# Value products of a head group: four places between score units, or one run behind the fifth unit

## The chip, the cores and the metric

The kernel runs on one NeuronCore of a Trainium2 chip. The metric is the device time of one execution in microseconds (us). The engines are called PE (TensorE, matmuls), PEld (its weight loads), DVE (VectorE), ACT (ScalarE), POOL (GpSimd) and SP (which here only issues DMAs).

## The reference

The input is 16 sequences of 512 rows of 256 floats. What is computed, cut to what matters for the change:

```
xn = layernorm(x)                                   # 16 x 512 x 256
q, k = low-rank projections of xn, 16 heads of 16   # each through rank 64
v = xn @ v_w.T + v_b
att = softmax(where(causal, q @ k.T / 4, min))      # per head, 512 x 512
y = (att @ v) @ o_w.T + o_b
x + y + ffn(xn)    # ffn: 8 experts, each picks its 128 best rows per sequence, silu MLP 256-512-256
```

## The kernel before

The program has two parts. The first does layernorm, attention and the ranking of rows for the experts (up to about 850 us of the span), the second the experts. The change is in the first part.

**Groups and slots.** The 16 sequences (b) have 4 head groups each (g), of 4 heads: 64 groups, G = 4b + g. The work is written out by hand as *slots*, one for each group; `slot_steps` (L56) lists the steps of a slot. All engines run through the same list of steps in the same order, and each does its own part of a step, held by semaphores. Two sequences (eight slots) are the body of a hardware loop (`program`, L338). In what follows "first" to "fourth slot" are g = 0 to 3 of one sequence, and four slots together are a *batch*.

**Units.** A slot has 10 units (u0 to u9). In each unit come, in this order: `scoret` of group G+1 (L877: transposed scores of 512 columns into one of two PSUM banks, which ACT turns into probabilities, L565, and of which POOL clears the diagonal blocks, L469), `score` of group G+3 (L858: scores of 512 columns into one of three PSUM banks, of which DVE takes row maxima, L719), then the steps that two hand-written tables give for that unit. `SUMS` (L49) has the steps of the softmax and the value products, `PROJECTIONS` (L39) the projections of this and later sequences. Those of `SUMS` come first in a unit.

**Waits of PE.** `score` of a unit waits until DVE has reduced the unit three before (L862, three banks). `scoret` waits until ACT has done the unit two before (L881). A shared pair of banks serves all other steps in turn (L797, `await_units` L780).

**Value products.** `pv` k (L892) multiplies the four heads' probabilities of key block k (128 keys, 512 - 128k query columns, fp32) by their values with a column of ones, each head on its own 32 columns of the PE array, and adds up in one PSUM bank over k = 0 to 3. Step 0 waits for POOL (L897) and for the copy of the group before (L903). Step 3 signals `pv_ready` (L913); ACT then copies the bank to `yraw` (L567 to L569), at the place of step 3 in its own list.

**Other steps in `SUMS`.** `maxt` (L870) transposes the negated row maxima of group G+2 on PE, also into 32 columns of the array, and ACT copies them. `maxd` (L553) is ACT's DMA of that copy. `ytr` (L914) transposes `yraw`; DVE normalises (L743, L749).

**Steps of `PROJECTIONS`.** `xt`, `qk_first`, `qk` (both L776), `v`, `yt`, `o` use PE, then ACT (upper half) and DVE (lower half, L588; for `o` the sum with the residual, L756). `mid` turns q and k into bf16 parts on ACT (L541) and POOL (L460), and SP stacks them by 6 DMAs for each of q and k (L400). Behind them SP loads x of a later sequence (`xload`, L382), for which DVE waits in `lnstat` (L655), the last step of the first slot. The first `score` of the second slot is the first that needs the new stack (L864).

Per unit, the steps with PE work besides the scores, `pv`, `maxt` and `ytr`: first slot u0 v, u1 yt, u6 yt, u8 v, u9 v; second u0 v, u2 o, u5 o, u6 o, u8 o; third u0 xt, u1 xt, u6 qk_first, u8 qk, u9 qk_first; fourth u0 qk, u4 qk_first, u6 qk, u8 qk_first, u9 qk.

The order inside one unit is this loop:

```
    for t in range(UN):
        out += [("scoret", G + 1, t)] * (G + 1 < NG) + [("score", G + 3, t)] * (G + 3 < NG) + put[t]
```

Of the kernel before, what the change touches and what calls it, by code (L numbers as in the profile page):

```python
# [25 lines left out]
def unit_parts(t, transposed):  # L26
# [20 lines left out]
     (8, "qk_first", 2, 3), (9, "qk", 2, 3)])  # L47

SUMS = (  # L49
# [4 lines left out]


def slot_steps(b, g):  # L56
# [1125 lines left out]
```

## Time and profile before

| | |
|---|---|
| median of 3 runs | 1301.3 us (1298.12 to 1302.88) |
| the profiled execution, its own time | 1300.67 us |
| its span, first to last instruction | 1298.8 us |
| mean granted TensorE clock | 0.972 of full speed |
| PE busy | 1196.6 us (92%) |
| DVE busy | 965.2 us (74%) |
| ACT busy | 669.8 us (52%) |
| POOL busy | 691.7 us (53%) |

The profile has a page of totals, and a trace that can be asked for stretches. A timeline row has the start in us from the beginning of the span, the duration in us, the engine, the source line, the operation, the tiles it writes and reads, shapes and number of instructions; in brackets the idle time of the engine before it and what ended it. PE's matmuls are pipelined: each row's duration includes the way through the array, so the time that an instruction costs PE is read from one start to the next, not from durations.

### The profile page before, as it was taken

The numbers are of one execution on the slowest core, as the hardware profiler recorded it, in microseconds if no ns is written. First come the engines' busy times: TensorE is split into PE (matmuls) and PEld (weight loads), VectorE is DVE, ScalarE is ACT, GpSimd is POOL, SyncE is SP. The second block draws the span as 40 slices with busy tenths as digits, with TensorE's granted clock in tenths as the row PEclk, the third lists the DMA queues.
The fourth block names the chain that finished last, engine by engine and source line by source line (L and its number), as shares of the span: only waits on it lengthen the run. The fifth ranks groups of instructions, "written<-read, shape, count | busy, mean of one in ns | idle before, by whom it ended". The sixth has DMA issues, their size and how long they took to land. (4 is left out here: it accounts for less than half of the span.)

```text
span 1298.8 us, 29459 instructions
## 1 busy us (share of the span) xinstructions
PE 1196.6 (92%) x8502; PEld 799.1 (62%) x8502; DVE 965.2 (74%) x3293; ACT 669.8 (52%) x1312; POOL 691.7 (53%) x1021
## 2 busy tenths in 40 slices
PE   6799999999999999999999998769999999999995
PEld 5544545555545555555555543348988888888885
DVE  3588878878878878878878879935766656666662
ACT  2357667667667667667667665522332323233220
POOL 1235354355354355345345343344888888888885
PEclk9779999999999999999999999969999999999998
DMA  5443443443443443443443442132555555555454
GB/s 140 114 115 83 116 115 100 116 115 98 114 115 98 114 115 98 114 115 98 114 115 98 114 98 67 34 109 42 108 101 93 117 88 107 93 101 109 85 78 53
DMA packets 106287, 130.31 MB, mean 100 GB/s; under 512 B 21580, under 2 KB 75476, under 8 KB 106196
## 3 DMA queue, kind: packets, MB, share of 16 engines
q1 hardware_dynamic: 76356, 94.46, 27.9%
q0 software_dynamic: 24576, 33.57, 15.7%
q10 hardware_dynamic: 5264, 1.32, 0.5%
q8 instruction: 27, 0.44, 0.1%
q14 instruction: 64, 0.52, 0.1%
HBM read 44.84 MB, written 33.55 MB: 60 GB/s over the span
## 5 line engine op out<-in xcount | busy, mean ns | idle before, releaser
L719 DVE CUSTOM_DVE_ANT_0 junk<-bank,rowmask 128x256 bf16<-128x256 f32 (+3 forms) x1024 | 454.3, 485 | 67.8 <-PE bank L866 42.2
L565 ACT ACTIVATE probs<-bank 128x512 f32<-128x512 f32 x640 | 376.6, 598 | 176.8 <-PE bank L887 175.5
L469 POOL TENSOR_SCALAR_AFFINE_SELECT probs<-probs 128x256 f32<-128x256 f32 (+1 forms) x640 | 223.6, 362 | 315.2 <-ACT probs L565 313.4
L866 PE MATMUL bank<-kstk,qstk 96*128 96x256 bf16 (+3 forms) x1024 | 250.3, 306 | 27.4 <-DMA kstk<-qk_part 13.4
L887 PE MATMUL bank<-qstk,kstk 98*128 98x256 bf16 (+3 forms) x1024 | 252.0, 308 | 3.4 <-ACT probs L565 2.4
L1049 POOL DMA_INDIRECT out_rows<-mixed,rows x128 | 208.5, 1629 | 58.2 <-issue 38.4
L908 PE MATMUL bank<-probs,vaug 128*32 128x512 f32 (+3 forms) x2048 | 193.8, 450 | 6.0 <-POOL probs L469 6.0
L1078 ACT ACTIVATE hid<-bank 128x512 f32<-128x512 f32 x128 | 76.5, 598 | 228.7 <-PE bank L1141 172.4
L887 PEld LDWEIGHTS bank<-qstk,kstk 98*128 98x128 bf16 x1024 | 76.6, 98 | 161.3 <-ACT probs L565 98.5
L1157 PE MATMUL bank<-w_hi,hid_hi 128*128 128x256 f32 x512 | 147.2, 288 | 0.0
L1157 PE MATMUL bank<-w_hi,hid_lo 128*128 128x256 f32 x512 | 144.9, 283 | 0.0
L1157 PE MATMUL bank<-w_lo,hid_hi 128*128 128x256 f32 x512 | 144.8, 283 | 0.0
L866 PEld LDWEIGHTS bank<-kstk,qstk 96*128 96x128 bf16 x1024 | 89.8, 99 | 65.6 <-DVE rowmax L719 26.2
L1109 DVE TENSOR_SCALAR mixed<-bank,gate_sel 128x256 f32<-128x256 f32 x128 | 56.1, 480 | 93.1 <-PE bank L1157 85.4
L460 POOL TENSOR_TENSOR qk_part<-rest,qk_part 128x512 bf16<-128x512 f32 x64 | 74.5, 1164 | 58.1 <-ACT qk_part L541 55.2
L1157 PEld LDWEIGHTS bank<-w_lo,hid_hi 128*128 128x128 f32 x512 | 98.2, 192 | 0.0
L1157 PEld LDWEIGHTS bank<-w_hi,hid_hi 128*128 128x128 f32 x512 | 98.1, 192 | 0.0
L1157 PEld LDWEIGHTS bank<-w_hi,hid_lo 128*128 128x128 f32 x512 | 98.1, 192 | 0.0
L1098 DVE CAST hid_hi<-hid 128x512 fp32r<-128x512 f32 x128 | 55.4, 433 | 49.7 <-ACT hid L1078 31.7
L1100 DVE TENSOR_TENSOR hid_lo<-hid,hid_hi 128x512 fp32r<-128x512 f32 x128 | 89.0, 695 | 4.4
L719 DVE DVE_READ_ACCUMULATOR2_ANT rowmax<- 128x1 f32 x1024 | 85.0, 83 | 0.0
L1141 PE MATMUL bank<-pt_hi,w_hi 128*128 128x512 f32 x256 | 81.0, 398 | 3.9 <-DVE pt_lo L1094 3.9
(131 smaller groups left out, 2060.5 us busy)
## 6 DMA issues: line engine op xcount, KB each, us to landing
qstk<-qk_part SPq DMA_DIRECT2D x96, 256.0 KB, 4.7
kstk<-qk_part SPq DMA_DIRECT2D x96, 256.0 KB, 4.7
xln<-in_L_attn_hidden_states SPq DMA_DIRECT2D x16, 512.0 KB, 6.1
xn_rows<-xn SPq DMA_DIRECT2D x16, 512.0 KB, 3.0
xres<-in_L_attn_hidden_states SPq DMA_DIRECT2D x16, 512.0 KB, 3.6
out_rows<-xres SPq DMA_DIRECT2D x16, 512.0 KB, 2.9
qstk<-in_L_ffn_w SPq DMA_DIRECT2D x8, 512.0 KB
kstk<-in_L_ffn_w SPq DMA_DIRECT2D x8, 512.0 KB
```

Of the source, the lines that this page charges most:

```text
L460: nc.gpsimd.tensor_tensor(qk_part[2][:, k, :], rest[k % 2][:], qk_part[1][:, k, :], ALU.subtract).then_inc(lo_done, 1)
L469: nc.gpsimd.affine_select(out=block, in_=block, compare_op=ALU.is_ge, fill=0.0, base=0, pattern=[[0, len(cols)], [1, P]], channel_multipli ...
L565: nc.scalar.activation(probs[n % 2][:, 512 * k:512 * k + 512], SCORET[k % 2][:], ACT.Exp, scale=SCALE).then_inc(exp_done, 1)
L719: last = nc.vector.tensor_tensor_reduce(out=junk[k % 2][:, col:col + width], in0=SCORE[score_bank(UN * n + k)][:, col:col + width], in1=ro ...
L866: last = nc.tensor.matmul(SCORE[score_bank(UN * n + k)][:, col:col + width], qstk[b % 2][0:KS, GH * g + h, P * i:P * i + P], kstk[b % 2][0 ...
L887: last = nc.tensor.matmul(SCORET[k % 2][:, col:col + width], kstk[b % 2][0:KS + SHIFT, GH * g + h, P * j:P * j + P], qstk[b % 2][0:KS + SH ...
L908: last = nc.tensor.matmul(Y[2 * HD * h:2 * HD * h + 2 * HD, P * k:T], vaug[b % 2][:, k, GH * g + h, :], probs[n % 2][:, col:col + width], ...
L1049: nc.gpsimd.indirect_dma_start(out=out_rows, out_offset=bass.IndirectOffsetOnAxis(ap=moe.rows[:, GB4 * grp + j, e:e + 1], axis=0), in_=mix ...
L1078: nc.scalar.activation(hid[k % 2][:], UP[k][:], ACT.Silu).then_inc(silu_done, 1)
L1100: nc.vector.tensor_tensor(hid_lo[n % 2][:, k, :], hid[k % 2][:], hid_hi[n % 2][:, k, :], ALU.subtract).then_inc(hid_done, 1)
L1141: last = nc.tensor.matmul(UP[k][:], a[:, dt, f], b[:, dt, :], start=m == 0 and dt == 0, stop=m == 2 and dt == DT - 1)
L1157: last = nc.tensor.matmul(DOWN[k][:, D * t:D * t + D], a, b, start=m == 0, stop=m == len(todo_mm) - 1)
```

## The change

Each of the four rows of `SUMS` belongs to one slot of a batch. The entry (unit, kind, groups ahead, k) says where a step stands. The change moves `pv` 0, 1 and 3; `pv` 2, `maxt`, `maxd` and `ytr` keep their units.

```
 SUMS = (
-    [(2, "pv", 0, 0), (3, "maxt", 2, 0), (3, "pv", 0, 1), (4, "maxd", 2, 0), (4, "pv", 0, 2), (5, "pv", 0, 3), (7, "ytr", 0, 0)],
-    [(2, "pv", 0, 0), (3, "maxt", 2, 0), (3, "pv", 0, 1), (4, "maxd", 2, 0), (4, "pv", 0, 2), (6, "pv", 0, 3), (7, "ytr", 0, 0)],
-    [(2, "pv", 0, 0), (3, "maxt", 2, 0), (3, "pv", 0, 1), (4, "maxd", 2, 0), (4, "pv", 0, 2), (5, "pv", 0, 3), (7, "ytr", 0, 0)],
-    [(2, "pv", 0, 0), (3, "maxt", 2, 0), (3, "pv", 0, 1), (4, "maxd", 2, 0), (4, "pv", 0, 2), (5, "pv", 0, 3), (7, "ytr", 0, 0)])
+    [(3, "maxt", 2, 0), (4, "pv", 0, 0), (4, "pv", 0, 1), (4, "maxd", 2, 0), (4, "pv", 0, 2), (4, "pv", 0, 3), (7, "ytr", 0, 0)],
+    (the same row three more times)
```

`maxd` has no PE part, so on PE the sixteen products of a group stand in one run behind the fifth score unit (u4). In the fourth slot `qk_first` of u4 follows the run. All waits stay as written.

## Rows read from the trace of the kernel before

**Rows 1.** The page: busy time, share of the span, instructions
```profile
PE 1196.6 (92%) x8502; PEld 799.1 (62%) x8502; DVE 965.2 (74%) x3293; ACT 669.8 (52%) x1312; POOL 691.7 (53%) x1021
```

**Rows 2.** Busy time by stretch: PE, PEld, DVE, ACT, POOL, granted clock, DMA
```profile
400.00:500.00 100.00, 97.24 (x759) 53.25 (x756) 85.04 (x351) 68.81 (x140) 43.99 (x95) 1.00 0.43 111
```

**Rows 3.** Who waited for whom, 100 to 740 us: total us, times, longest
```profile
PE bank L866 <- DMA kstk<-qk_part: 11.0, 10, 1.6
PE bank L866 <- DVE rowmax L719: 5.2, 6, 1.1
```

**Rows 4.** Timeline of PE, third slot of a batch, u2 to u6
```profile
445.43 0.38 PE L866 MATMUL bank<-kstk,qstk 96*128 96x256 bf16 x2
445.74 1.07 PE L908 MATMUL bank<-probs,vaug 128*32 128x512 f32 x8
446.74 0.39 PE L887 MATMUL bank<-qstk,kstk 98*128 98x512 bf16 x1
446.96 0.38 PE L866 MATMUL bank<-kstk,qstk 96*128 96x512 bf16 x1
447.28 0.23 PE L874 MATMUL bank<-ident_bf,negmax 128*32 128x128 bf16 x1
447.29 0.86 PE L908 MATMUL bank<-probs,vaug 128*32 128x384 f32 x8
448.08 0.39 PE L887 MATMUL bank<-qstk,kstk 98*128 98x384 bf16 x2
...
449.74 0.43 PE L908 MATMUL bank<-probs,vaug 128*32 128x128 f32 x8
450.09 0.39 PE L887 MATMUL bank<-qstk,kstk 98*128 98x384 bf16 x2
```

**Rows 5.** Timeline of DVE, third slot: end of u0, end of u1, u2, u5
```profile
446.36 0.08 DVE L719 DVE_READ_ACCUMULATOR2_ANT rowmax<- 128x1 f32 x1
...
447.65 0.08 DVE L719 DVE_READ_ACCUMULATOR2_ANT rowmax<- 128x1 f32 x1
...
448.25 0.41 DVE L719 CUSTOM_DVE_ANT_0 junk<-bank,rowmask 128x256 bf16<-128x256 f32 x1
...
450.23 0.68 DVE L719 CUSTOM_DVE_ANT_0 junk<-bank,rowmask 128x512 bf16<-128x512 f32 x1
```

**Rows 6.** Timeline of PE and DVE, fourth slot, u2 to u6
```profile
407.93 0.38 PE L866 MATMUL bank<-kstk,qstk 96*128 96x256 bf16 x2
...
408.64 0.08 DVE L719 DVE_READ_ACCUMULATOR2_ANT rowmax<- 128x1 f32 x1
...
409.93 0.08 DVE L719 DVE_READ_ACCUMULATOR2_ANT rowmax<- 128x1 f32 x1
...
411.13 0.64 PE L908 MATMUL bank<-probs,vaug 128*32 128x256 f32 x8
...
411.70 0.50 PE L776 MATMUL bank<-xt_hi,wqk_hi 128*128 128x512 f32 x1
...
412.51 0.39 PE L887 MATMUL bank<-qstk,kstk 98*128 98x512 bf16 x1
...
413.33 0.69 DVE L719 CUSTOM_DVE_ANT_0 junk<-bank,rowmask 128x512 bf16<-128x512 f32 x1 [1.14 <-PE bank L866]
413.40 0.39 PE L887 MATMUL bank<-qstk,kstk 98*128 98x384 bf16 x2
```

**Rows 7.** Timeline, boundary from first to second slot: PE, then DVE
```profile
431.66 0.39 PE L866 MATMUL bank<-kstk,qstk 96*128 96x512 bf16 x1 [1.26 <-DMA kstk<-qk_part]
...
432.71 0.75 DVE L657 BATCH_NORM_STATS2 stats<-xln 128x6 f32<-128x256 f32 x2 [1.81 <-DMA xln<-in_L_attn_hidden_states]
```

**Rows 8.** Timeline, first slot at a turn of the loop: DVE u0, PE u3, DVE u5
```profile
471.15 0.69 DVE L719 CUSTOM_DVE_ANT_0 junk<-bank,rowmask 128x512 bf16<-128x512 f32 x1 [2.76 <-issue]
...
471.90 0.39 PE L866 MATMUL bank<-kstk,qstk 96*128 96x512 bf16 x1 [1.05 <-DVE rowmax L719]
...
475.04 0.69 DVE L719 CUSTOM_DVE_ANT_0 junk<-bank,rowmask 128x512 bf16<-128x512 f32 x1
```

3 rows, old and new, of the table SUMS are left out of this document.

## The prediction

> **What bounds the kernel now.** I began with the page. PE is busy 92% of the span, DVE 74% [rows 1]. That is an average over two parts, so I asked for stretches. Within the attention part PE is busy 97 of 100 us and DVE 85, at full granted clock [rows 2]. The experts' part isn't touched, and I leave it at what it takes.
>
> Next I read who waited for whom. Between 100 and 740 us PE waits 5.2 us for DVE's row maxima and 11.0 us for the stack DMA (ten waits, of at most 1.6 us) [rows 3]. So PE sets the pace almost everywhere, and once per batch a transfer does. But DVE has only 15% to spare and feeds back on PE through three score banks. The question is whether PE still finds a free bank when the order changes, and that has to be read from timelines.
>
> I followed one batch: third slot [rows 4, 5], fourth slot [rows 6], the boundary between first and second [rows 7], and a first slot at a turn of the loop [rows 8]. The reader should see there how late DVE runs: the u3 score starts at 446.96, and the reduction of u0, whose bank it takes, ended only at 446.44 [rows 4, 5].
>
> **What the change removes on PE.** Starts are compared. A block of products costs 1.00, 0.79 and 0.35 us for 512, 384 and 128 columns [rows 4], 0.57 for 256 [rows 6]. The last two differ by 128 columns and 0.22, so streaming is close to 1.7 ns a column, 0.85, 0.64, 0.43 and 0.21 us, together 2.13; about 0.15 us remains at the end of each block. At the beginning, the score before a block costs 0.31 [rows 4], where a bf16 unit of 512 columns costs 0.22 (446.74 to 446.96) [rows 4]: 0.09 more. Where `qk_first` follows a block of 256 columns, it starts 0.57 after it, and the next scoret comes 0.81 later [rows 6]: 1.38 less 0.43 of streaming leaves 0.95 for exit and `qk_first` together.
>
> PE enters and leaves the narrow shape (32 columns a head) four times per slot now. `maxt` shares one of these stretches: it starts 0.01 before pv 1 [rows 4]. Afterwards `maxt` stands alone (0.09 + 0.05 of streaming + 0.15 = 0.29) and the run is one stretch (0.09 + 2.13 + 0.15, and I add 0.03 for three inner boundaries = 2.40). Old: 4 x 0.24 + 2.13 + 0.01 = 3.10. New: 2.69. **PE has 0.4 us per slot less to do.** The trace has no boundary between two blocks of products. Its cost lies between 0.01 (maxt to pv 1, same shape) and 0.15 (the full exit). I take 0.01, as the nearest row is one within the narrow shape, and keep 0.15 for the range.
>
> The Trainium skill, TensorEngine Tiling (Array Packing), section Tiling Modes, says that a change of tiling mode drains TensorE. By that rule alone the change only gains; the 0.09 and 0.15 above agree with it. It is the first rival's mechanism below.
>
> **What else moves.** No DMA moves, and SP and POOL keep their lists. The select that pv 0 waited for has two more units of time. On ACT the `yraw` copy now stands right after the exponential of u4 (behind `maxd`, which stays ahead of it) and waits for the run's end, with the exponential of u5 behind it. That costs nothing: scoret of u5 comes after the run anyway, and the first waiter is scoret of u7, over 1.2 us after the run; an ACT operation takes 0.51 on average (669.8 / 1312) [rows 1]. If u6 had no projection as cover, it could cost some 0.2 a slot.
>
> **What the change adds: PE meets the banks early, then starves DVE.** Third slot, both engines taken to start as before (in the second slot DVE is behind from its wait for x [rows 7], works without a break, and `o` and `ytr` wait for it, so PE can't gain there).
> - Scoret of u3 starts at 445.43 + 0.22 = 445.65, its score could start at 445.87, but needs u0's reduction, 446.44 [rows 5] plus 0.06 (the release seen in [rows 8], 471.84 to 471.90) = 446.50. **Stall 0.6.**
> - The score ends at 446.72, maxt alone 447.01, scoret of u4 447.24. The score of u4 needs u1's reduction, 447.73 + 0.06 = 447.79 [rows 5]. **Stall 0.55.** It ends at 448.01.
> - The run ends at 450.41, and u5 at 450.86. Before, u6 started at 450.09 [rows 4]. **PE is 0.77 late.**
> - DVE needs 1.98 us for u2 to u4 (448.25 to 450.23) [rows 5], is done at 450.23 and gets u5 at about 451.2, so it idles 1 us where it had none. From u5 on PE works through without a stall, as before, so all that follows is 0.7 to 0.8 late.
>
> Fourth slot, everything 0.77 later:
> - scoret of u3 at 407.93 + 0.22 + 0.77 = 408.92, the score wanted at 409.15, allowed at 408.72 + 0.77 + 0.06 = 409.55 [rows 6] (stall 0.4); maxt ends 410.06; the score of u4 wanted at 410.29, allowed at 410.01 + 0.83 = 410.84 (stall 0.55), done 411.06.
> - The run without its exit takes 2.25, exit and `qk_first` 0.95, u5 0.45: u6 starts at 414.7 instead of 413.40 [rows 6]. That is 1.3 late in all. PE is seldom as exactly placed as in a sum of starts, and only a reading that errs towards a stall is hidden in it, so **I take 1.2 per batch.** DVE's idle time before u5 grows from 1.14 [rows 6] to over 2.
>
> First and second slot. The split of the last `qk` of the fourth slot is what `mid`, the stack DMAs and the load of x follow from. It is 1.2 late, so the stack and x arrive 1.2 late [rows 7]. PE and DVE waited 1.26 and 1.81 there, which covers what the run does within the first slot (PE gains 0.4 and waits it again). So the batch grows by 1.2, not by more. In the second slot DVE is behind from its wait for x, and the run costs it nothing. At a turn of the loop DVE starts 2.76 late and PE waits 1.05 [rows 8]: there u5's score comes at 471.90 + 0.22 + 0.29 + 0.45 + 2.40 + 0.23 = 475.5, and DVE starts it at 476.1 instead of 475.04, so 1.0 late. The wait for x covers some of it: 1.81 in [rows 7], but less here, where DVE starts late; I take 0.65 and leave 0.35.
>
> **Sum.** 14 sequences with the whole structure (b = 0 to 13; the last two have no `qk` left) x 1.2 = 16.8; 6 turns of the loop x 0.35 = 2.1; the last two sequences about 1 (DVE has rank steps between u3, u4 and u5, which fill most of the gap). Together **+20 us**. The profiled execution took 1300.67 us and the median is 1301.3, 0.6 above, so the forecast for the median is **1321 us** (+1.5%).
>
> **Rivals.**
> 1. *Faster: PE keeps what the fewer exits give.* Decides if DVE's reductions of u0 and u1 end before PE wants their banks, or if DVE catches up. Per batch, the last three slots gain 0.4 each, the first nothing for its DMA: 14 x 1.2 = 17 less, 1284 us. For it: PE is busy 97%, DVE 85% [rows 2]. Against it: DVE's times in [rows 5, 6] leave PE 0.5 us of room at u3, and the change takes away pv 0 ahead of it, 1.1 us with its entry. Chance 0.10.
> 2. *No change.* The stalls are there, but DVE's lateness is caught up in gaps of the fourth and first slot (1.26 at the DMA alone [rows 7]), if the stack isn't as late as the split. Then stalls and gain cancel: 1301 us. Against it: between u5 of the fourth slot and the stack everything hangs on PE's own order. Chance 0.13.
> 3. *Slower still: inner boundaries cost 0.15 each.* The run takes 2.82 instead of 2.40, in third and fourth slot (0.84 a batch, 12 us) and, 0.2 each, at the loop's turns (1 us): 1334 us. For it: weights of the next block's four heads can't be seen loading ahead in the trace. Against it: [rows 4], maxt to pv 1. Chance 0.15.
>
> The forecast has 0.62. Half a per cent, 6.5 us, is about what a measurement of this kernel can tell. Slower by more than that: forecast and rival 3, 0.77, and a small part of rival 2, so 0.78. Within it: 0.12. Faster: rival 1, 0.10. The forecast's own range, with 0.15 to 0.2 us of reading error in each stall, is 1311 to 1330. The range goes to 1303 below, into rival 2, and to 1336 above, over rival 3. Rival 1 and half of rival 2 stay out.
>
> **What the new profile would show.** PE: in the third slot the u3 and u4 scores each with an idle time before them that ends by DVE, about 0.5 us; the total "PE waits for DVE row maxima" up from 5 us to some 25 to 30 (13 batches x 2.1). The run's four blocks 2.4 us from first start to next scoret; 2.8 means rival 3. DVE: idle 1 us before u5 in the third slot and 2 in the fourth. The wait for the stack DMA no shorter than now. A batch 1.2 us longer than now. The forecast is wrong if the stalls at u3 and u4 are missing, or if they are there and the next batch's stack still lands at the old pace. The experts' part should not change.

## The result and the profile after

| | before | after |
|---|---|---|
| median | 1301.4 us (4 runs) | 1344.99 us (1342.63 to 1347.15, 4 runs) |
| ratio | | 1.034, 95% interval 1.0315 to 1.0364 |
| span of the profiled execution | 1298.8 us | 1345.2 us |
| mean granted clock | 0.972 | 0.958 |
| us lost to a clock under full, from the first `ytr` to the last | 6.8 | 25.6 |

The change costs 44 us, where 20 were forecast: the sign was right, the size less than half. (The last row sums one less the granted clock over the time. From the first to the last `ytr` is nearly all of the attention part.)

The page after. The second line is the granted clock in tenths, in 40 slices; it answers to [rows 1] with its busy times.

```profile
PE 1193.4 (89%) x8502; PEld 833.3 (62%) x8502; DVE 962.8 (72%) x3293; ACT 660.8 (49%) x1312; POOL 691.6 (51%) x1021
...
PEclk9779999999999989999999998877999999999998
```

PE does the same instructions in 3 us less busy time, in a span 46 us longer. The stretch that answers to [rows 2]:

```profile
400.00:500.00 100.00, 91.09 (x695) 52.74 (x694) 76.59 (x317) 61.64 (x128) 42.06 (x90) 0.95 0.41 103
```

PE fell from 97 to 91 us of 100, DVE from 85 to 77, and the clock is no longer full. What PE waited for between 100 and 740 us (answers to [rows 3]):

```profile
PE bank L887 <- ACT probs L565: 20.6, 34, 0.8
PE bank L866 <- DVE rowmax L719: 17.9, 21, 2.3
PE bank L866 <- DMA kstk<-qk_part: 8.8, 7, 1.8
```

The waits for DVE came, 18 us for 5, though fewer than the 25 to 30 that the prediction looked for. The largest wait is one that [rows 3] hasn't: `scoret` waits 20.6 us for ACT's exponentials (2.4 us in the whole kernel before).

The third slot, PE (answers to [rows 4]), from scoret of u3 to scoret of u5, and then DVE at u5 (answers to [rows 5]):

```profile
412.48 0.39 PE L887 MATMUL bank<-qstk,kstk 98*128 98x512 bf16 x1
413.32 0.39 PE L866 MATMUL bank<-kstk,qstk 96*128 96x512 bf16 x1 [0.45 <-DVE rowmax L719]
414.00 0.22 PE L874 MATMUL bank<-ident_bf,negmax 128*32 128x128 bf16 x1 [0.28 <-DVE xt_lo L588]
414.16 0.39 PE L887 MATMUL bank<-qstk,kstk 98*128 98x384 bf16 x2
414.61 0.39 PE L866 MATMUL bank<-kstk,qstk 96*128 96x384 bf16 x2
414.93 2.36 PE L908 MATMUL bank<-probs,vaug 128*32 128x512 f32 x32
417.23 0.39 PE L887 MATMUL bank<-qstk,kstk 98*128 98x512 bf16 x1
```
```profile
418.05 0.69 DVE L719 CUSTOM_DVE_ANT_0 junk<-bank,rowmask 128x512 bf16<-128x512 f32 x1 [0.91 <-PE bank L866]
```

The score of u3 could have started 0.22 after its scoret, at 412.70, and started at 413.32: 0.6 late, as forecast. The idle time in brackets is shorter than the delay, since the matmul before is still shown running for a part of it. The run takes 2.30 us to the next scoret, DVE idles 0.91 before u5 (1 forecast). This slot went as worked out.

The fourth slot (answers to [rows 6]), PE from the u2 score to the u5 scoret:

```profile
423.91 0.38 PE L866 MATMUL bank<-kstk,qstk 96*128 96x256 bf16 x2
425.09 0.39 PE L887 MATMUL bank<-qstk,kstk 98*128 98x512 bf16 x1 [0.80 <-ACT probs L565]
425.32 0.38 PE L866 MATMUL bank<-kstk,qstk 96*128 96x512 bf16 x1
425.63 0.23 PE L874 MATMUL bank<-ident_bf,negmax 128*32 128x128 bf16 x1
426.36 0.39 PE L887 MATMUL bank<-qstk,kstk 98*128 98x384 bf16 x2 [0.50 <-ACT probs L565]
426.59 0.43 PE L866 MATMUL bank<-kstk,qstk 96*128 96x384 bf16 x2
426.94 3.95 PE L908 MATMUL bank<-probs,vaug 128*32 128x512 f32 x32
430.83 0.50 PE L776 MATMUL bank<-xt_hi,wqk_hi 128*128 128x512 f32 x1
```

Two things differ from the forecast. The scoret of u3 was due at 424.13 (0.22 after the score before it) and comes 0.96 later, that of u4 was due at 425.79 (0.16 after `maxt`, as in the third slot) and comes 0.57 later, both held by ACT. And the run takes 3.89 us to the next row, not the 2.3 that it takes in the third slot and in ten of the fourteen fourth slots. ACT in that time:

```profile
423.43 0.60 ACT L537 ACTIVATE qk_part<-bank 128x512 bf16<-128x512 f32 x1 [0.31 <-PE bank L776]
423.93 0.62 ACT L541 ACTIVATE qk_part<-rest 128x512 bf16<-128x512 f32 x1
424.45 0.59 ACT L565 ACTIVATE probs<-bank 128x512 f32<-128x512 f32 x1
425.19 0.63 ACT L541 ACTIVATE qk_part<-rest 128x512 bf16<-128x512 f32 x1 [0.15 <-DVE rest L588]
425.73 1.07 ACT L565 ACTIVATE probs<-bank 128x512 f32<-128x512 f32 x2
```

The exponential of u1 (424.45), whose bank scoret of u3 needs, stands behind the split of the projection and the copy of `mid`; that of u2 (425.73) behind a second copy. In the kernel before, ACT's order was the same and PE didn't wait, because pv 0 stood ahead of the scoret of u3 and gave ACT the time. There (fourth slot of [rows 6]) the exponential of u1 ends at 409.06, and that scoret follows at 409.24 without idle time:

```profile
408.47 0.59 ACT L565 ACTIVATE probs<-bank 128x512 f32<-128x512 f32 x1
409.24 0.39 PE L887 MATMUL bank<-qstk,kstk 98*128 98x512 bf16 x1
```

The granted clock around that run, by stretches of 1 us (after the length: PE, PEld, DVE, ACT, POOL, clock, DMA):

```profile
424.00:425.00 1.00, 0.29 (x3) 0.01 (x1) 1.00 (x3) 1.00 (x3) 0.37 (x1) 1.00 0.00 0
425.00:426.00 1.00, 0.77 (x3) 0.27 (x3) 1.00 (x6) 0.85 (x3) 1.00 (x2) 1.00 0.00 0
426.00:427.00 1.00, 0.64 (x8) 0.32 (x12) 1.00 (x5) 1.00 (x4) 1.00 (x2) 0.90 0.00 0
427.00:428.00 1.00, 1.00 (x9) 0.34 (x12) 0.91 (x6) 0.41 (x1) 1.00 (x4) 0.50 0.00 0
428.00:429.00 1.00, 1.00 (x12) 0.20 (x4) 0.01 (x2) 0.00 (x0) 0.25 (x1) 0.50 0.30 68
429.00:430.00 1.00, 1.00 (x12) 0.26 (x8) 0.00 (x0) 0.00 (x0) 0.00 (x0) 0.50 0.98 297
```

PE idles 1.3 of 3 us in these waits, and then the clock is at its lower level, 0.50 (1.2 GHz), through most of the run, the densest work there is. It doesn't happen each time: PE idles 1.2 to 1.3 us in the 4 us before the run in all fourth slots of the first fourteen sequences, and 4 of these 14 runs met the low clock. So did one run in a first slot and five of the seven last ones. Why just these isn't known.

DVE meanwhile has no score for 4.45 us, and the waits at the boundary between first and second slot (answers to [rows 7]) are only 0.15 us shorter than they were:

```profile
432.46 0.69 DVE L719 CUSTOM_DVE_ANT_0 junk<-bank,rowmask 128x512 bf16<-128x512 f32 x1 [4.45 <-PE bank L866]
...
451.36 0.75 DVE L657 BATCH_NORM_STATS2 stats<-xln 128x6 f32<-128x256 f32 x2 [1.66 <-DMA xln<-in_L_attn_hidden_states]
```
```profile
450.30 0.39 PE L866 MATMUL bank<-kstk,qstk 96*128 96x512 bf16 x1 [1.11 <-DMA kstk<-qk_part]
```

**Pace.** From the timelines I took when PE starts `ytr` in each of the 64 slots, and the steps between these starts. Typical values of slots without a clock drop, us (the last two lines are experiments that come below):

```
                                 4th>1st  1st>2nd  2nd>3rd  3rd>4th   batch
before          loop not turning   11.64    14.47    10.56    11.76   48.4
                loop turning       12.8     13.4     10.51    11.74   48.5
after           loop not turning   11.73    14.25    11.33    12.78   50.1
                loop turning       13.36    13.04    11.26    12.78   50.4
run behind u2   loop not turning   11.57    14.86    10.42    11.24   48.1
mid at u3       loop not turning   11.73    14.28    11.33    12.10   49.4
```

A batch is 1.7 us longer at full clock, 2.0 at a turn of the loop, 7 x 1.66 + 7 x 1.99 = 25.6 us. With the clock drops, the first fourteen sequences are 37.6 us longer (716.0 for 678.4, first `ytr` to the first of the fifteenth), the last two 9.1 (89.4 for 80.2). The low clock lost (in the sense of the table's last row) 11.9 us in the first of these stretches, where it lost nothing before, and 13.7 in the second, for 6.8 before. So in the first stretch 12.0 us are left beyond the 25.6, and the clock has 11.9 for them. One of these drops, at 143.5 us, isn't at a run; it comes within 1 us of a wait of 1.78 us for the stack DMA.

### The profile page after: what moved, and what is told of

Same layout as the page of the kernel before. It is cut to its first block and busy times, and to the rows that moved or that the text cites. A ratio compares the mean times of both kernels' runs of the same rounds, so it can differ in the third digit from the quotient of the medians.

```text
span 1345.2 us, 29459 instructions
## 1 busy us (share of the span) xinstructions
PE 1193.4 (89%) x8502; PEld 833.3 (62%) x8502; DVE 962.8 (72%) x3293; ACT 660.8 (49%) x1312; POOL 691.6 (51%) x1021
## 5 line engine op out<-in xcount | busy, mean ns | idle before, releaser
L565 ACT ACTIVATE probs<-bank 128x512 f32<-128x512 f32 x640 | 367.5, 599 | 80.1 <-PE bank L887 79.0
L908 PE MATMUL bank<-probs,vaug 128*32 128x512 f32 (+3 forms) x2048 | 168.5, 474 | 4.9 <-POOL probs L469 4.9
L887 PEld LDWEIGHTS bank<-qstk,kstk 98*128 98x128 bf16 x1024 | 79.8, 99 | 111.7 <-ACT probs L565 54.7
L908 PEld LDWEIGHTS bank<-probs,vaug 128*32 128x32 f32 x2048 | 63.9, 117 | 106.4 <-issue 90.4
L569 ACT ACTIVATE yraw<-bank 128x512 f32<-128x512 f32 x64 | 38.3, 598 | 151.2 <-PE bank L908 151.2
```

The source lines that it names most:

```text
L565: nc.scalar.activation(probs[n % 2][:, 512 * k:512 * k + 512], SCORET[k % 2][:], ACT.Exp, scale=SCALE).then_inc(exp_done, 1)
L887: last = nc.tensor.matmul(SCORET[k % 2][:, col:col + width], kstk[b % 2][0:KS + SHIFT, GH * g + h, P * j:P * j + P], qstk[b % 2][0:KS + SH ...
L908: last = nc.tensor.matmul(Y[2 * HD * h:2 * HD * h + 2 * HD, P * k:T], vaug[b % 2][:, k, GH * g + h, :], probs[n % 2][:, col:col + width], ...
```

## Experiments

Theory A, after this reading: PE meets u3 and u4 too early, waits there for DVE and (fourth slot) ACT, and this idle time lets the clock fall in runs behind it. The rival theories (B to E) stand in the expectations. Medians below are to be held against 1345.0 us for the changed kernel. Fillers are extra matmuls that PE runs in its waits: their result is overwritten, and all outputs are still computed.

**One slot's row taken back.** The edits put the old row of `SUMS` back at its place:

```
e1_fourth_back:     rows new, new, new, old
e2_third_back:      rows new, new, old, new
e3_first_two_back:  rows old, old, new, new
```

> Only the fourth slot gets its old row back; the other three keep the run behind u4. Theory A (two causes: PE stalls on DVE and ACT around u3 and u4, and in the fourth slot the clock falls to half during the run, since PE stood idle just before it): in the changed kernel's trace the step from the third to the fourth slot's ytr is 1.0 us longer than before, and in four of fourteen batches 2.6 us. Taking that back gives 14 x 1.0 + 4 x 1.6 = 20 us and some of the clock losses at the end, about 1320 to 1325 us. Theory B (the run as such is dearer than four blocks, in every slot alike): a quarter of 44 us, about 1334 us. Theory C (my prediction's reading, stalls of the third and fourth slot only at full clock, 1.3 against 0.8): about 1337 us.

Measured: 1327.2 us, ratio 1.0206 (1.0183 to 1.0229): 18 us back by one slot of four. Theory B, equal shares (1334 us), is out, and so is theory C, the prediction's own reading (1337 us).

> Only the third slot gets its old row back. Theory A: the step from second to third slot's ytr is 0.7 us longer in the changed kernel, 14 x 0.7 = 10 us, so about 1333 to 1336 us, with the clock drops of the fourth slot still there. Theory B: 1334 us as well, so this run alone does not part A from B; with the run before it does. Theory C: 14 x 0.8 = 11 us, 1334 us.

Measured: 1341.6 us, 1.0313 (1.0293 to 1.0332), a miss for all: 3 us back, not 10. The step from second to third slot is 10.5 again. But the clock now fell in seven fourth slots of the first fourteen sequences (3rd>4th at 14.4 to 14.6 instead of 12.8) and in two first slots. In these sequences it lost 18.8 us, for 11.9 in the changed kernel. What the third slot gave, 14 x 0.75 = 10.5 us, went to the clock for the most part. So the effects of single slots don't add up.

> First and second slot get their old rows back, third and fourth keep the run. Theory A: DVE's and PE's waits for the stack DMA and for x cover these two slots except where the loop turns (0.55 us longer, 6 times, and one clock drop of two windows there), so 3 to 7 us less: 1338 to 1342 us. Theory B: half of 44 us less, about 1323 us.

Measured: 1342.8 us, 1.0312 (1.0295 to 1.033). Theory B (1323 us) is out, and theory A's range is missed by 0.8 us. The first two slots are covered: at full clock a batch takes 50.2 us, for 50.1 and 50.4 in the changed kernel. The clock fell in six fourth slots here.

**Fillers: is it the clock?** The numbers of fillers per place are given in the expectations; `filler` looks them up.

```
+  if filler(kind, n, k):
+      pe.wait_ge(yraw_done, at(n - 3, 8))          # n - 1 ahead of scoret
+  for _ in range(filler(kind, n, k)):
+      nc.tensor.matmul(Y[:], wqk_hi[:, 0, 0:P], wqk_hi[:, 0, :], start=True, stop=True)
```

> All four rows as in the changed kernel. PE runs 2 to 6 matmuls whose result nobody reads (512 columns fp32r, into the bank of the value products before pv 0 clears it) ahead of the waits at u3 and u4: in the third slot before the scores, in the fourth before scoret, and before the u3 score of the first slot at a turn of the loop. They fill time in which PE waits anyway, and cost PE time where the wait is shorter. Theory A: with PE busy before the run the granted clock stays at full speed in the runs of the steady batches (in the changed kernel five of them fell to half), which is worth 1.6 us each time, 8 us, less what the fillers push back (up to 0.3 us a slot, 28 slots, 8 us): 1330 to 1345 us, and no run longer than 2.4 us between 100 and 780 us. Theory B and C: no effect on the length of a run; the time is that of the changed kernel or longer.

Measured: 1345.2 us, 1.0331 (1.0313 to 1.0348). All fourth slots take 12.8 us now and no run between 100 and 780 us meets the low clock, as theory A has it. But the third slot pays 0.3 for its fillers (11.57 for 11.27), 4 us, and one step from first to second slot early on, with the low clock in it, takes 17.2 us for 15.1. In the trace the first fourteen sequences are only 1.5 us shorter (714.5 for 716.0), and the last two are as long as in the changed kernel. So the mechanism is there and the sum is nil, 0.2 us above theory A's range. Without the costly fillers:

> The changed kernel with fillers only in the fourth slot (3 matmuls before scoret of u3, 2 before scoret of u4) and 6 before the u3 score of the first slot at a turn of the loop; none in the third slot, where they cost 0.3 us a slot in the run before. The fourth slot took 12.8 us from ytr to ytr in every batch with fillers, as in the changed kernel without a clock drop, so there they cost nothing. Theory A: the changed kernel less its clock drops in the steady part (five, some with two windows, 1.6 us each): 1333 to 1339 us. If the clock is not what made the long runs dear, 1345 us as the changed kernel.

Measured: 1337.5 us, 1.0285 (1.0257 to 1.0313), in theory A's range. 7.5 us back by nothing but extra work on the busiest engine. In its trace the clock lost 5.1 us in the first fourteen sequences, for 11.9, and they take 710.8 us, for 716.0. What PE waits for in that kernel, 100 to 740 us (its lines are shifted: L904 is scoret, L879 score):

```profile
PE bank L879 <- DVE rowmax L728: 10.5, 20, 0.9
...
PE bank L904 <- ACT probs L574: 3.2, 7, 0.5
```

The waits for ACT fell from 20.6 to 3.2 us, and a fourth slot without a clock drop takes 12.8 us as before: the fillers stand in the waits, at no cost, and all that changed there is the clock. In the three kernels that have these fillers (this one, the one before and `e16_tail_fill` below) none of 42 such runs in fourth slots met the low clock, for 4 of 14 in the changed kernel and 7 of 14 with the third slot taken back.

**ACT's list.**

```
-    ... (0, "mid", 2, 0), (1, "mid", 2, 1), ...     # fourth row of PROJECTIONS
+    ... (3, "mid", 2, 0), (3, "mid", 2, 1), ...
```

> The changed kernel with one more move: in the fourth slot both mid steps (two ACT copies of 0.6 us, two POOL subtractions, the 6 stack DMAs of q) go from u0 and u1 to u3. Theory A: the waits of scoret at u3 and u4 (0.96 and 0.5 us) come from ACT's list, where these copies stand ahead of the exponentials of u1 and u2. Without them PE waits there only for DVE (0.4 and 0.55 us): the fourth slot falls from 12.8 to 12.2-12.4 us, 14 x 0.5 = 7 us, and with less idle time the clock falls less often: 1328 to 1340 us. If DVE alone sets these waits (my prediction's reading): 1345 us. The q stack lands some 2 us later, which must not matter as the k stack lands last.

Measured: 1338.8 us, 1.029 (1.0259 to 1.0322). The fourth slot falls from 12.78 to 12.10 in nearly every batch, 9.5 us; 6 us arrive. Theory A holds, and DVE alone (1345 us) doesn't explain the waits. Part of the gain is lost at five turns of the loop, where the step to the first slot takes 15.6 to 16.9 us instead of 13.4. Two things are behind this: the clock fell in these first slots, and DVE now idles 3.4 to 3.6 us at the turn, for 2.6 to 2.9 in the changed kernel (the wait that [rows 8] show with 2.76 us and `issue`). Why the move makes DVE later there isn't known. PE in one of its fourth slots: the score waits for DVE now, at 422.46, and scoret hardly for ACT.

```profile
421.14 0.39 PE L887 MATMUL bank<-qstk,kstk 98*128 98x512 bf16 x1 [0.28 <-ACT probs L565]
422.46 0.39 PE L866 MATMUL bank<-kstk,qstk 96*128 96x384 bf16 x2 [0.23 <-DVE rowmax L719]
```

**Does DVE's hunger cost by itself?**

```
-    ... (4, "qk_first", 2, 2), ...     # fourth row of PROJECTIONS
+    ... (5, "qk_first", 2, 2), ...
```

> The changed kernel with qk_first of the fourth slot moved from u4 (behind the run) to u5. DVE then gets the u5 score 0.8 us earlier, so its longest idle time (4.5 us in a run at half clock, about 2.7 otherwise) shrinks by 0.8 us. Theory A: PE works without a stall from the run to the end of the slot and sets the time, so DVE's idle time there costs nothing and the time stays within 3 us of 1345 us. Theory D (what costs is that DVE starves in the run and is late afterwards): 14 x 0.8 = 11 us less, 1334 us.

Measured: 1347.2 us, 1.0372 (1.034 to 1.0404). No gain. DVE's longest idle time costs nothing by itself; PE sets the pace behind the run. Theory D (1334 us) is out.

**The same run elsewhere.**

```
e4_run_at_u2, all four rows:
+    [(2, "pv", 0, 0), (2, "pv", 0, 1), (2, "pv", 0, 2), (2, "pv", 0, 3), (3, "maxt", 2, 0), (4, "maxd", 2, 0), (7, "ytr", 0, 0)]
```

> The same run of four blocks, but behind u2, where pv 0 stood before; maxt stays at u3 and stands alone. Theory A (the place of the run does the harm: at u4 PE has taken the free score banks and exponentials before it and stalls; the shape changes that the run saves are real): PE reaches the u3 and u4 scores after the run, when DVE and ACT are through with u0 to u2, so no stalls there, no clock drops in the runs, and PE has 0.4 us per slot less to do. DVE gets no score for 2.7 us, but at u2 it is 1 to 2 us behind. Third and fourth slot 0.2 to 0.4 us shorter than in the kernel before, first and second covered by their waits: 1290 to 1303 us. Theory B (a run of 2.4 us as such is dear, wherever it stands): 1330 to 1345 us.

Measured: 1300.5 us beside 1300.1 before, ratio 1.0009 (0.9996 to 1.0021). The whole loss is gone by moving the same run two units up. What PE waits for, 100 to 740 us:

```profile
PE bank L866 <- DMA kstk<-qk_part: 13.0, 13, 2.1
...
PE bank L866 <- DVE rowmax L719: 3.9, 7, 0.8
```

No wait for an exponential, DVE's as low as before, and no clock drop between 100 and 780 us. The saved shape changes are real (3rd>4th 11.24 for 11.76), but the way from the fourth slot's end over the stack DMA got 0.3 us longer and takes half of it back (batch 48.1 for 48.4). The first fourteen sequences are 3.6 us shorter than in the kernel before (674.8 for 678.4), the last two 2.5 us longer (82.7 for 80.2).

```
e10_run_u3, all four rows:
+    [(3, "maxt", 2, 0), (3, "pv", 0, 0), (3, "pv", 0, 1), (3, "pv", 0, 2), (3, "pv", 0, 3), (4, "maxd", 2, 0), (7, "ytr", 0, 0)]
```

> The run one unit earlier, behind u3, with maxt directly ahead of it in the same unit, so that maxt needs no stretch of its own; maxd at u4 as before. Theory A (place decides): in the third slot the u3 score still meets a bank that DVE frees 0.6 us later, and in the fourth u3 waits for the exponential, but u4 stands behind the run and never waits. So about half of the stalls of the changed kernel (0.55 and 0.5 to 0.55 us less in third and fourth slot, 15 us in 14 batches) and most clock drops go: 1308 to 1320 us. Theory B (any run costs) is already out by the run at u2.

Measured: 1334.7 us, 1.0268 (1.0239 to 1.0297). A miss: one unit earlier helps by 10 us, not 30. The fourth slot fell to 11.96, but the second to third stayed at 11.3 to 11.4, the first to second got longer (14.7 for 14.3), and so did the first slot at a turn (4th>1st 13.6, and 15.3 with the low clock). So it matters to be ahead of u3's wait, and of the places tried only u2 is.

```
e12_two_pairs, all four rows:
+    [(2, "pv", 0, 0), (2, "pv", 0, 1), (3, "maxt", 2, 0), (4, "maxd", 2, 0), (4, "pv", 0, 2), (4, "pv", 0, 3), (7, "ytr", 0, 0)]
```

> Two runs of two blocks, pv 0 and 1 behind u2, pv 2 and 3 behind u4, maxt alone at u3: three narrow stretches a slot where the kernel before has four. Theory A: pv 0 and 1 (1.6 us) now stand ahead of the u3 score, so no new stall there; DVE is never without a score for longer than 1.4 us. PE has some 0.2 us per slot less to do, of which the waits for stack and x keep the part of the first two slots: 1294 to 1301 us, same or a little faster than before.

Measured: 1304.9 us, 1.0027 (1.0006 to 1.0048). A narrow miss: the fourth slot takes 11.5 us, less than before. But the step from first to second slot takes 17.3, 16.9 and 15.5 us in the second to fourth sequence (14.8, 14.9 and 14.5 before), with two clock drops there, and the last two sequences are 3.3 us longer. What starts this is open.

**A version that beats both.**

```
e14_u2_mid_early: e4_run_at_u2 and, in the first row of PROJECTIONS,
-    (0, "v", 1, 0), (1, "mid", 1, 3), (1, "yt", -1, 0), ...
+    (0, "v", 1, 0), (0, "mid", 1, 3), (1, "yt", -1, 0), ...
```

> A version meant to beat both kernels: the run behind u2, and the last mid of the first slot from u1 to u0, so that ACT's copy stands ahead of the exponential of u1 and the k stack starts about 0.5 us earlier. With the run at u2 the second to fourth slot got 0.15, 0.5 and 0.1 us shorter per batch, but the way from the fourth slot's end to the stack 0.3 us longer, and PE waits 1.0 us for the stack in every batch. If that DMA chain is what sets the time there, 14 x 0.4 = 6 us less: 1293 to 1297 us. If v at u0 or DVE's split sets it instead: 1300 us.

Measured: 1297.3 us (12 runs) beside 1301.0 (23 runs), ratio 0.997 (0.9955 to 0.9985): 3.7 us faster than the kernel before, at the upper end of what was expected. 1st>2nd goes from 14.86 (with the run behind u2) to 14.39, so the DMA chain sets the time there.

**What was left open: turns of the loop and the end.**

> The changed kernel with mid of the fourth slot at u3 (as two runs before) and fillers only ahead of the u3 score of the first slot at a turn of the loop, where in that run the clock fell in five batches. Theory A: both gains add up. The fourth slot takes 12.1 us, the first slot at a turn 13.4 instead of 15.9 us: two sequences take 99.4 us instead of 102 (97.0 in the kernel before). From 1338.8 us five times 2.5 us less, 1325 to 1330 us. If the clock is beside the point there, 1338 us or more.

Measured: 1338.0 us, 1.0278 (1.0248 to 1.0309), a miss. In its trace PE still idles behind the fillers, and at three turns the run that follows meets the low clock:

```profile
487.04 1.75 PE L873 MATMUL bank<-wqk_hi 128*128 128x512 f32 x6
...
490.34 0.39 PE L879 MATMUL bank<-kstk,qstk 96*128 96x512 bf16 x1 [1.55 <-DVE rowmax L728]
...
491.36 3.80 PE L921 MATMUL bank<-probs,vaug 128*32 128x512 f32 x32
```

> The kernel with mid at u3 and fillers at the turn of the loop, with 13 of them ahead of the u3 score instead of 6. With 6, PE still idled 1.55 us before that score and the clock fell in the run behind it in three of the steady batches (338 us missed the forecast). Theory A: 13 matmuls at 0.24 us cover the 3 us that PE waits there, the clock stays, and the first slot at a turn takes 13.4 us from the fourth slot's ytr instead of 15.9: 1326 to 1332 us. If DVE's late start at the turn and not the clock makes this slot long: 1338 us, with the clock at full speed.

Measured: 1335.2 us, 1.0272 (1.0253 to 1.0291), above the expected range. The part on the clock came true: it stays up at all turns, and the runs take 2.3 us:

```profile
381.72 3.32 PE L873 MATMUL bank<-wqk_hi 128*128 128x512 f32 x13
...
384.29 0.69 DVE L728 CUSTOM_DVE_ANT_0 junk<-bank,rowmask 128x512 bf16<-128x512 f32 x1 [3.59 <-issue]
...
386.07 2.36 PE L921 MATMUL bank<-probs,vaug 128*32 128x512 f32 x32
```

But the step from the fourth slot is 14.3 us, not 13.4. The fillers aren't the reason, as it is 14.3 also at the two turns of the run before that kept the clock, with 6 fillers. It is DVE, which starts 0.9 us later at a turn in all three kernels with `mid` at u3 (3.6 us idle, for 2.7). So both readings of the expectation hold in part: the clock made the slot dearer than 14.3, and DVE's late start makes it 14.3.

> The changed kernel with fillers in fourth slots and at the turn of the loop (1337.5 us) and, new, ahead of the scores of u1 to u4 in the last seven groups (57 to 60), where PE waits for DVE 0.3 to 1.3 us before each. There the clock fell in each run: 2.6 to 4.5 us a run instead of 2.4. Theory A: the clock is what makes the last two sequences 9 us longer than before; with PE busy in the waits the runs there take 2.4 us and the time falls by 4 to 7 us, to 1331 to 1334 us. Theory E (DVE, which has the ranking there as well, sets the pace, and a run at half clock lies beside its backlog): 1336 to 1339 us, though the runs are short.

Measured: 1333.0 us, 1.0245 (1.0226 to 1.0264), as theory A has it: 4.5 us less than with fillers in the steady part alone. The intervals of the two overlap a little, but the traces agree: the last two sequences take 84.3 us, for 88.0, and the clock lost 5.1 us in them, for 17.1. (The expectation says that the clock fell in each of these runs; it was three of four.) The run of one of the last groups, first without (`e7_fill_fourth`) and then with fillers in the last sequences:

```profile
825.72 4.12 PE L925 MATMUL bank<-probs,vaug 128*32 128x512 f32 x32
```
```profile
826.96 2.36 PE L927 MATMUL bank<-probs,vaug 128*32 128x512 f32 x32
```

## Why the prediction was right in sign and wrong in size

**What held.** PE's saving and the shape changes: the run takes 2.30 us to the next scoret, so inner boundaries cost next to nothing (2.30 less 0.15 and 2.13 leaves 0.02). Rival 3 is out by this, though its 1334 us lie nearer to the result than the forecast. The third slot: stalls of 0.62 at u3 and 0.58 from there to u4's score (0.36 of it at `maxt`, whose bank DVE still held) for 0.6 and 0.55, and 0.7 to 0.8 late, for 0.77. A turn of the loop: the change adds 0.3 us more there than to another batch, for 0.35. The first two slots are covered, and the stack comes late with the split, 0.15 us nearer to it than before (rivals 1 and 2 are out). The run at u2 kept PE's saving in third and fourth slot, so it was the stalls that took it at u4. DVE's idle time costs nothing, as taken.

**What failed, first: in the fourth slot, "the score wanted at 409.15, allowed at 408.72 + 0.77 + 0.06 = 409.55 [rows 6] (stall 0.4)".** The step held the score against DVE and never held `scoret` against ACT: that wait was put at nothing, without a reason. The condition was in the code (two banks, exponential of two units before), and ACT's list in the fourth slot has three more operations ahead of the exponentials of u1 and u2. With them the delays are 0.96 and 0.57, in sum 0.6 more than the 0.4 and 0.55 taken; 3rd>4th grew by 1.0, where the forecast had 1.3 less 0.77, 0.5. That is 0.5 x 14 = 7 us. Moving the two copies gave 0.68 per batch and left the fourth slot 0.34 us longer than before the change (12.10 for 11.76), so without ACT the step of the prediction comes out nearly right. I had looked at ACT only behind the run.

**Second: full clock in every sum.** [rows 2] show it for the kernel before, and it was carried over to a kernel to which I had just given 2 us more idle time per batch, directly ahead of its densest stretch. Fillers that keep PE busy gave back 7.5 us, and those in the last two sequences 4.5 us more, 12 us in all. They didn't remove every drop. The trace of the changed kernel says what the low clock lost beyond the kernel before: 11.9 us in the first fourteen sequences and 6.9 in the last two. The Trainium skill (TensorE: Matmul & The Clock Gate, section HAM oscillation) tells of a kernel in which long waits for a DMA bring the clock down, so that the matmuls behind each wait start at the lower clock. The traces here agree in direction, with shorter waits: 0.80 and 0.50 us idle in 3 us, and a run of 3.89 instead of 2.3 us behind them, in some of many equal places.

**Third: "the last two sequences about 1".** They cost 9.1 us. The reading was that DVE's ranking steps fill most of the gap, and it left out that the clock falls there. The fillers gave back about half of it (4.5 us), and the clock lost 6.9 us more there than in the kernel before, so most of it is the clock.

Together, by the two traces, first to last `ytr`: 19.9 forecast, plus 6.7 (ACT; 25.6 at full clock, less the 16.8 and 2.1 forecast), plus 12.0 (clock, first fourteen sequences), plus 8.1 (last two sequences, up to 6.9 of it the clock), is 46.7 us. The profiled executions are 46.4 us apart, the medians 44. Shown by experiment are ACT's part and 12 us of the clock's. Of the other 8 us beyond the forecast the granted clock accounts for up to 6.8; no run shows this, and 1 us stays unexplained. It is open why the clock falls at some of the equal places and not at others.

## What to carry to other kernels

When work that stood ahead of a wait is moved behind it, every wait that follows has to be held against its releaser again, on each engine that releases one. That goes for waits that had room to spare before, too. In this kernel a dense run does no harm ahead of the waits, where it gives the other engines time, and much behind them: the same sixteen products cost 44 us behind u4 and nothing behind u2. And once a change gives PE new idle time ahead of dense matmuls, the clock belongs in the sum.

## What the runs showed of the hardware

- Useless matmuls made a kernel faster: five of 0.24 us in the fourth slot's waits of 1.5 us and six at each turn of the loop, and the time fell from 1345.0 to 1337.5 us.
- The clock fell in some of many equal places: 4 of 14 fourth slots with the same waits. With the third slot restored it fell in seven. So undoing one part of a harm can give much less than that part costs (3 us of 10).
- Between blocks of the same narrow shape PE loses about 0.01 us (0.02 for the three boundaries of the run), on entering it 0.09, by [rows 4], and on leaving 0.15. The last also comes out without the estimate for streaming: four blocks apart cost 2.71 us, in one run 2.30, so three exits are 0.41.
